# Transposing c2q alone: a change to the cross attention of a decoder layer on one core

## The chip, the core and the metric

The kernel runs on one core of a Trainium2 chip. The metric is device time in microseconds (us), the median of the runs made. A core has five engines with a queue each: TensorE (PE; its weight loads are listed apart as PEld), VectorE (DVE), ScalarE (ACT), GpSimd (POOL) and SyncE (SP), which here issues all DMAs. Each works through its instructions in the order in which they are written, and waits at semaphores.

## What is computed

A decoder layer in float32 over x (32 batches, 112 tokens, width 256) and a context (32 batches, 375 rows, width 256): self attention over channels, a cross attention, and a mixture of eight experts with a shared one. The change is in the cross attention, cut here to its core (c is the normalised state, q the context):

```python
cq = jnp.einsum('bcd,bqd,d->bcq', c, q, w_cq) + b_cq
s = (c @ w_c + b_c)[:, :, None] + (q @ w_q + b_q)[:, None, :] + cq
a = jax.nn.softmax(s, axis=2)
c2q_att = jnp.einsum('bcq,bqd->bcd', a, q)
b_att = jax.nn.softmax(jnp.max(s, axis=2), axis=1)
q2c_att = jnp.einsum('bc,bcd->bd', b_att, c)[:, None, :]
x = jnp.concatenate([c, c2q_att, c * c2q_att, c * q2c_att], axis=-1)
z = x @ W_l.T + b_l
```

## The kernel before

The kernel has two stages. The first runs both attentions in eight groups of four batches; a batch of a group is called a stream, j = 0 to 3. The first and the last group are written out, the six between are a loop, so they run the same instructions. The second stage runs the experts over blocks of 512 tokens; the change doesn't touch it.

Every float32 product is made of three in a faster type: each operand is split into a high part (a rounded copy, made by ScalarE) and a low part (the operand minus its high part, made by VectorE, for the context by GpSimd), and `mm3` (lines 74 to 78) takes low x high, high x low and high x high. So an operand passes through a bank of PSUM, ScalarE, VectorE and back to TensorE.

The order on each engine is written out by hand in that engine's `group`. At the end of a group this is done for each stream:

- `c2q_product` (L487, line numbers L76 to L78 in the trace, tiles ctx_hi, ctx_lo and op_hi, op_lo): the attention weights by the context, 9 products of 256 columns, into the stream's bank.
- L751 on ScalarE: c2q is scaled by the sum of exponentials and copied into `tmp`. L1126 on VectorE: c2q times c, into the other half of `tmp` (semaphore `x3_ok`, c_c2q_ready).
- `turn_x` (L499): four transposes of 128 columns each, of c2q and of c*c2q, into the stream's bank. L759 and L1138: high and low part of all four, 448 columns in one instruction each.
- `z_c2q` (L502): 12 products of 256 columns with two of the four blocks of W_l, added up in `z_bank`.

Between them stand other steps. `turn_h_pair` (L374) transposes the next group's normalised input hh, which VectorE makes in `normalise_h` (L921). The b_att chain goes over the four streams: m4, a transpose (L556), its maximum (L1121), the exponential (L754), `mrow` (L1133), a transpose back (L565), `b4` (L1142), and then eight small products (L571) that give q2c. ScalarE has `residual` (L602, four activations for the next group) between the last `a_high` (L679) and the first copy of c2q, and `context_hi` (L608, L609) of the next group's first stream after the second L759. GpSimd waits for the last x3_ok and then makes the low parts of that context (L822, L827). The last group has no next one: it has no `residual` and no `turn_h_pair`, but `moments3` (L147 to L156, the next stage's norm) on VectorE.

`c` transposed is kept in `ct`, as [128, stream, 2, 112], since z's first block needs it.

Of the kernel before, what the change touches and what calls it, by code (L numbers as in the profile page):

```python
# [26 lines left out]
ALU = mybir.AluOpType  # L27
# [23 lines left out]
def decoder_layer(nc, x, ctx, ctx_t, norm_w, norm_b, qkv_wt, qk_b, v_b, proj_wt, proj_b, w_cq, b_cq, w_c, b_c,  # L51
# [29 lines left out]
    with outer:  # L81
# [102 lines left out]
        with ExitStack() as c1:  # L184
# [94 lines left out]
            c2q_mm, c2q_ok, x3_ok = sem("c2q_product"), sem("c2q_copied"), sem("c_c2q_ready")  # L279
            t_x, x_hi_ok, x_lo_ok = sem("x23_transposed"), sem("x23_hi_ready"), sem("x23_lo_ready")  # L280
# [81 lines left out]
            def _(pe):  # L362
# [39 lines left out]
                def group(i, last_group):  # L402
# [93 lines left out]
                    def turn_x(j):  # L496
                        pe.wait_ge(x3_ok, ev[j])
                        for k in range(2 * KB):
                            last = pe.transpose(bank[j][:, k * L:(k + 1) * L], tmp[j][0:L, k * P:(k + 1) * P], ident[0:L, 0:L])  # L499
                        last.then_inc(t_x, 1)  # L500

                    def z_c2q(j):  # L502
                        pe.wait_ge(x_lo_ok, ev[j])
                        for k in range(2 * KB):
# [69 lines left out]
                    z_c2q(1)  # L574
# [3 lines left out]
                    z_c2q(2)  # L578
                    z_c2q(3)
                    if last_group:  # L580
# [13 lines left out]
            def _(act):  # L594
# [30 lines left out]
                def group(i, last):  # L625
# [50 lines left out]

                    def a_high(j):
# [70 lines left out]
                    for j in range(G):  # L748
                        act.wait_ge(c2q_mm, ev[j])
                        act.wait_ge(sinv2_ok, ev[j])  # L750
                        act.activation(tmp[j][0:L, 0:D], bank[j][0:L, 0:D], ACT.Copy, scale=sinv2[:, j:j + 1]).then_inc(c2q_ok, 1)  # L751
                        if j == 2:
                            act.wait_ge(mneg_ok, i + 1)
                            act.activation(mexp[:, :], m_bank[0:G, 0:L], ACT.Exp, bias=mneg[:, :], accum_out=msum[:, :]).then_inc(mexp_ok, 1)  # L754
                    if not last:
                        h_high_pair(i + 1, 0)
                    for j in range(G):
                        act.wait_ge(t_x, ev[j])
                        act.activation(op_hi[j][:, 0:2 * KB * L], bank[j][:, 0:2 * KB * L], ACT.Copy).then_inc(x_hi_ok, 1)  # L759
                        if j == 1 and not last:  # L760
                            context_hi(i + 1, 0)
                        if j == 1 and last:
                            act.wait_ge(shared_in, 48)
                            act.activation(shared_hi[:, 0:GU + D], shared_f[:, :], ACT.Copy).then_inc(shared_hi_ok, 1)
# [137 lines left out]
            def _(dve):  # L902
# [39 lines left out]
                def group(i, last):  # L942
# [33 lines left out]

                    def a_low(j):
# [146 lines left out]
                    for j in range(G):  # L1124
                        dve.wait_ge(c2q_ok, ev[j])
                        dve.tensor_tensor(tmp[j][0:L, D:2 * D], tmp[j][0:L, 0:D], c[:, j, :], ALU.mult).then_inc(x3_ok, 1)  # L1126
                        if j == 0 and last:
                            moments3(dve, 0)
                        if j == 2:
                            dve.wait_ge(mexp_ok, i + 1)  # L1130
                            dve.reciprocal(minv[:, :], msum[:, :]).then_inc(minv_ok, 1)
                            dve.wait_ge(minv_ok, i + 1)
                            dve.tensor_scalar(mrow[:, :], mexp[:, :], minv[:, 0:1], None, ALU.mult).then_inc(mrow_ok, 1)  # L1133
                    if not last:
                        h_low_pair(i + 1, 0)
                    for j in range(G):
# [471 lines left out]
```

## Time and profile before

| | us |
|---|---|
| median of 3 runs | 758.57 |
| lowest, highest | 756.07, 758.85 |
| the profiled execution, its time | 759.8 |
| its span, first to last instruction | 758.0 |
| TensorE busy in it | 699.2 |
| VectorE, ScalarE, GpSimd busy | 500.4, 408.3, 347.4 |

Busy times of different engines overlap. A product on TensorE is listed with its latency (0.28 us for 256 columns), but the next one starts 0.117 us later, so the distance of starts is its cost in the queue. An idle time stands in brackets with the instruction that ended it.

### The profile page before, as it was taken

The numbers are of one execution on the slowest core, as the hardware profiler recorded it, in microseconds if no ns is written. First come the engines' busy times: TensorE is split into PE (matmuls) and PEld (weight loads), VectorE is DVE, ScalarE is ACT, GpSimd is POOL, SyncE is SP. The second block draws the span as 40 slices with busy tenths as digits, with TensorE's granted clock in tenths as the row PEclk, the third lists the DMA queues.
The fourth block names the chain that finished last, engine by engine and source line by source line (L and its number), as shares of the span: only waits on it lengthen the run. The fifth ranks groups of instructions, "written<-read, shape, count | busy, mean of one in ns | idle before, by whom it ended". The sixth has DMA issues, their size and how long they took to land. (4 is left out here: it accounts for less than half of the span.)

```text
span 758.0 us, 13311 instructions
## 1 busy us (share of the span) xinstructions
PE 699.2 (92%) x4496; PEld 616.8 (81%) x4496; DVE 500.4 (66%) x1232; ACT 408.3 (54%) x923; POOL 347.4 (46%) x482
## 2 busy tenths in 40 slices
PE   3879999999999999999999865989999999999997
PEld 2768888988988898889888854878888888888886
DVE  5686685775875866758758654766576667666442
ACT  4855766776776768567767532524243333333321
POOL 2756846765657558557575311323222223232222
PEclk9989999999999999999999998999999999999999
DMA  7622322313213313223001057022221203121200
GB/s 215 180 87 69 117 69 66 108 38 98 88 48 88 98 47 99 65 70 117 24 22 37 18 148 266 1 112 83 112 84 58 108 31 138 55 112 57 112 29 29
DMA packets 50769, 64.47 MB, mean 85 GB/s; under 512 B 3801, under 2 KB 49417, under 8 KB 49841
## 3 DMA queue, kind: packets, MB, share of 16 engines
q1 hardware_dynamic: 50736, 64.06, 26.7%
q8 instruction: 18, 0.29, 0.2%
q14 instruction: 15, 0.11, 0.0%
HBM read 56.60 MB, written 7.45 MB: 85 GB/s over the span
## 5 line engine op out<-in xcount | busy, mean ns | idle before, releaser
L1440 POOL TENSOR_TENSOR sg<-sg,cw_wide 128x512 f32<-128x512 f32 x56 | 74.6, 1331 | 187.9 <-ACT sg L1397 177.7
L1401 ACT ACTIVATE a_hi<-af 128x512 fp32r<-128x512 f32 x63 | 39.8, 632 | 157.4 <-DVE af L1521 157.4
L76 PE MATMUL bank<-h_hi,w_lo 128*128 128x512 f32 x224 | 92.6, 413 | 6.9 <-DVE w_lo L1538 5.1
L77 PE MATMUL bank<-h_lo,w_hi 128*128 128x512 f32 x224 | 90.5, 404 | 0.0
L78 PE MATMUL bank<-h_hi,w_hi 128*128 128x512 f32 x224 | 89.6, 400 | 0.0
L822 POOL TENSOR_TENSOR ctxt_lo<-ctxtf,ctxt_hi 128x375 fp32r<-128x375 f32 x64 | 58.4, 933 | 64.3 <-ACT ctx_hi L609 56.2
L1521 DVE TENSOR_TENSOR af<-bank,sg 128x512 f32<-128x512 f32 x63 | 43.2, 686 | 65.0 <-POOL sg L1440 61.9
L1526 DVE TENSOR_TENSOR a_lo<-af,a_hi 128x512 fp32r<-128x512 f32 x63 | 47.2, 749 | 34.9 <-ACT a_hi L1401 34.9
L827 POOL TENSOR_TENSOR ctx_lo<-ctxf,ctx_hi 125x256 fp32r<-125x256 f32 x96 | 68.9, 746 | 0.0
L76 PE MATMUL bank<-w_hi,a_lo 128*128 128x256 f32 x224 | 63.3, 283 | 0.0
L77 PE MATMUL bank<-w_lo,a_hi 128*128 128x256 f32 x224 | 63.2, 282 | 0.0
L78 PE MATMUL bank<-w_hi,a_hi 128*128 128x256 f32 x224 | 63.2, 282 | 0.0
L76 PEld LDWEIGHTS bank<-h_hi,w_lo 128*128 128x128 f32 x224 | 43.4, 194 | 17.9 <-DVE w_lo L1538 5.5
L78 PEld LDWEIGHTS bank<-h_hi,w_hi 128*128 128x128 f32 x224 | 43.6, 195 | 10.2
L77 PEld LDWEIGHTS bank<-h_lo,w_hi 128*128 128x128 f32 x224 | 43.7, 195 | 7.8
L1003 DVE TENSOR_TENSOR op_lo<-bank,op_hi 112x512 fp32r<-112x512 f32 x32 | 22.1, 692 | 36.5 <-ACT op_hi L630 36.5
L1397 ACT ACTIVATE sg<-bank 128x512 f32<-128x512 f32 x63 | 37.1, 589 | 14.2 <-PE bank L78 13.9
L76 PEld LDWEIGHTS bank<-w_hi,a_lo 128*128 128x128 f32 x224 | 42.5, 190 | 2.5 <-DVE a_lo L1526 0.2
L77 PEld LDWEIGHTS bank<-w_lo,a_hi 128*128 128x128 f32 x224 | 42.6, 190 | 2.3
L78 PEld LDWEIGHTS bank<-w_hi,a_hi 128*128 128x128 f32 x224 | 42.6, 190 | 0.0
L76 PE MATMUL bank<-wp_hi,op_lo 128*128 128x256 f32 x128 | 38.5, 301 | 2.3 <-DVE wp_lo L1044 1.5
L76 PE MATMUL bank<-wl_hi,op_lo 128*112 128x256 f32 x128 | 37.8, 296 | 1.1 <-DVE op_lo L1138 1.1
(252 smaller groups left out, 2293.3 us busy)
## 6 DMA issues: line engine op xcount, KB each, us to landing
cw_wide<-cw_scratch SPq DMA_DIRECT2D x7, 2048.0 KB, 7.1
ctxtf<-in_ctx_t SPq DMA_DIRECT2D x32, 375.0 KB
ctxf<-in_ctx SPq DMA_DIRECT2D x32, 375.0 KB
xt<-in_x SPq DMA_DIRECT2D x8, 448.0 KB, 3.7
x_scratch<-x2b SPq DMA_DIRECT2D x8, 448.0 KB, 3.2
x2n<-x_scratch SPq DMA_DIRECT2D x7, 512.0 KB, 4.7
x2t<-x_scratch SPq DMA_DIRECT2D x7, 512.0 KB, 3.9
out_dram<-x2t SPq DMA_DIRECT2D x7, 512.0 KB, 2.9
```

The lines of the kernel that those rows point to most:

```text
L76: pe.matmul(dst, a_lo, b_hi, start=first, stop=False, **kw)
L77: pe.matmul(dst, a_hi, b_lo, start=False, stop=False, **kw)
L78: return pe.matmul(dst, a_hi, b_hi, start=False, stop=last, **kw)
L822: last_lo = pool.tensor_tensor(ctxt_lo[:, j, k, 0:S], ctxtf[:, j, k, :], f32(ctxt_hi[:, j, k, 0:S]), ALU.subtract)
L827: last_lo = pool.tensor_tensor(ctx_lo[:, j, b, :], ctxf[0:SB, j, b, :], f32(ctx_hi[:, j, b, :]), ALU.subtract)
L1003: dve.tensor_tensor(op_lo[j][0:L, :], bank[j][0:L, :], f32(op_hi[j][0:L, :]), ALU.subtract).then_inc(qk_lo_ok, 1)
L1397: act.activation(sg[b][:, :], g_bank[b][:, :], ACT.Silu).then_inc(sg_ok, 1)
L1401: act.activation(a_hi[n % (AHEAD + 1)][:, :], af[(p + n) % 2][:, :], ACT.Copy).then_inc(a_hi_ok, 1)
L1440: pool.tensor_tensor(sg[b][:, :], sg[b][:, :], cw_wide[p][:, ORDER[n], :], ALU.mult).then_inc(sgw_ok, 1)
L1521: dve.tensor_tensor(af[b][:, :], u_bank[b][:, :], sg[b][:, :], ALU.mult).then_inc(af_ok, 1)
L1526: dve.tensor_tensor(a_lo[b][:, :], af[(p + n) % 2][:, :], f32(a_hi[b][:, :]), ALU.subtract).then_inc(a_lo_ok, 1)
```

## The change

Only c2q is transposed (two transposes per stream). c*c2q is then made by VectorE from the transposed c2q in the bank and `ct`, straight in the transposed layout. Its high and low part are instructions of their own, from `tmp`, and `z_c2q` is divided into `z_c2q` and `z_x3` with six products each. GpSimd's wait for x3_ok stays as it was written. The order on TensorE, ScalarE and VectorE is written anew.

```diff
                     def turn_x(j):
-                        pe.wait_ge(x3_ok, ev[j])
-                        for k in range(2 * KB):
+                        pe.wait_ge(c2q_ok, ev[j])
+                        for k in range(KB):
                             last = pe.transpose(bank[j][:, k * L:(k + 1) * L], tmp[j][0:L, k * P:(k + 1) * P], ident[0:L, 0:L])
...
+                    def z_x3(j):
+                        pe.wait_ge(x3_lo_ok, ev[j])
+                        for k in range(KB, 2 * KB):
...
                     c2q_product(2)
+                    turn_x(0)
                     c2q_product(3)
+                    turn_x(1)
                     if not last_group:
                         turn_h_pair(i + 1, 0)
-                    turn_x(0)
-                    turn_x(1)
+                    z_c2q(0)
+                    turn_x(2)
                     pe.wait_ge(mrow_ok, i + 1)
-                    turn_x(2)
+                    turn_x(3)
                     pe.transpose(m_bank[0:L, P:P + G], mrow[:, :], ident[0:G, 0:G]).then_inc(t_b, 1)
-                    turn_x(3)
-                    z_c2q(0)
+                    z_c2q(1)
+                    z_x3(0)
                     pe.wait_ge(b4_ok, i + 1)
...
-                    z_c2q(1)
+                    z_c2q(2)
+                    z_x3(1)
                     if not last_group:
                         pe.wait_ge(h_lo_ok, G * (i + 1) + 2)
                         turn_h_pair(i + 1, 1)
-                    z_c2q(2)
                     z_c2q(3)
+                    z_x3(2)
+                    z_x3(3)
...
+                    def c2q_copy(j):
+                        act.wait_ge(c2q_mm, ev[j])
+                        act.wait_ge(sinv2_ok, ev[j])
+                        act.activation(tmp[j][0:L, 0:D], bank[j][0:L, 0:D], ACT.Copy, scale=sinv2[:, j:j + 1]).then_inc(c2q_ok, 1)
+
+                    def x_high(j):
+                        act.wait_ge(t_x, ev[j])
+                        act.activation(op_hi[j][:, 0:KB * L], bank[j][:, 0:KB * L], ACT.Copy).then_inc(x_hi_ok, 1)
+
+                    def x3_high(j):
+                        act.wait_ge(x3_ok, ev[j])
+                        act.activation(op_hi[j][:, KB * L:2 * KB * L], tmp[j][:, D:D + KB * L], ACT.Copy).then_inc(x3_hi_ok, 1)
...
+                    c2q_copy(0)
+                    c2q_copy(1)
+                    x_high(0)
+                    c2q_copy(2)
+                    act.wait_ge(mneg_ok, i + 1)
+                    act.activation(mexp[:, :], m_bank[0:G, 0:L], ACT.Exp, bias=mneg[:, :], accum_out=msum[:, :]).then_inc(mexp_ok, 1)
+                    x_high(1)
+                    c2q_copy(3)
                     if not last:
                         h_high_pair(i + 1, 0)
...
+                    x3_high(0)
+                    x_high(2)
+                    x3_high(1)
+                    x_high(3)
+                    if not last:
+                        context_hi(i + 1, 0)
...
+                    x3_high(2)
+                    x3_high(3)
...
+                    def x_low(j):
+                        dve.wait_ge(x_hi_ok, ev[j])
+                        dve.tensor_tensor(op_lo[j][:, 0:KB * L], bank[j][:, 0:KB * L], f32(op_hi[j][:, 0:KB * L]),
+                                          ALU.subtract).then_inc(x_lo_ok, 1)
+
+                    def x3_product(j):
+                        dve.wait_ge(x_hi_ok, ev[j])
+                        dve.tensor_tensor(tmp[j][:, D:D + KB * L].rearrange("p (k t) -> p k t", k=KB),
+                                          bank[j][:, 0:KB * L].rearrange("p (k t) -> p k t", k=KB), ct[:, j, :, :], ALU.mult).then_inc(x3_ok, 1)
+
+                    def x3_low(j):
+                        dve.wait_ge(x3_hi_ok, ev[j])
...
+                    x_low(0)
+                    x3_product(0)
+                    if last:
+                        moments3(dve, 0)
+                    dve.wait_ge(mexp_ok, i + 1)
+                    dve.reciprocal(minv[:, :], msum[:, :]).then_inc(minv_ok, 1)
+                    x_low(1)
+                    dve.wait_ge(minv_ok, i + 1)
+                    dve.tensor_scalar(mrow[:, :], mexp[:, :], minv[:, 0:1], None, ALU.mult).then_inc(mrow_ok, 1)
+                    x3_product(1)
                     if not last:
                         h_low_pair(i + 1, 0)
...
+                    x3_low(0)
+                    x_low(2)
+                    x3_product(2)
+                    dve.wait_ge(t_b, i + 1)
+                    dve.tensor_copy(b4[:, :], m_bank[0:L, P:P + G]).then_inc(b4_ok, 1)
+                    x3_low(1)
+                    x_low(3)
+                    x3_product(3)
+                    x3_low(2)
+                    x3_low(3)
```

In these pieces the name in brackets is the semaphore that the instruction waits for (a_transposed is `t_a`, c2q_copied `c2q_ok`, c_c2q_ready `x3_ok`, b_att_rows `mrow_ok`, x23_lo_ready `x_lo_ok` before and c2q_lo_ready the same after). TensorE in the loop's group before, from the last context product of stream 3 to the first weight product:

```order
L78 MATMUL bank3<-ctx_hi,op_hi3 112x256
L370 REGISTER_ALU
L374 MATMUL bank7<-ident,h3 128x112 [waits hh_ready]
L374 MATMUL bank7<-ident,h3 128x112 x3
L499 MATMUL bank0<-ident,tmp 128x112 [waits c_c2q_ready]
L499 MATMUL bank0<-ident,tmp 128x112 x3
L499 MATMUL bank1<-ident,tmp 128x112 [waits c_c2q_ready]
L499 MATMUL bank1<-ident,tmp 128x112 x3
L499 MATMUL bank2<-ident,tmp 128x112 [waits c_c2q_ready,b_att_rows]
```

TensorE there after the change, from the last context product of stream 2:

```order
L78 MATMUL bank2<-ctx_hi,op_hi2 112x256
L500 MATMUL bank0<-ident,tmp 128x112 [waits c2q_copied]
L500 MATMUL bank0<-ident,tmp 128x112
L76 MATMUL bank3<-ctx_hi,op_lo3 112x256 [waits a_lo_ready,context_lo_ready]
...
L78 MATMUL bank3<-ctx_hi,op_hi3 112x256
L500 MATMUL bank1<-ident,tmp 128x112 [waits c2q_copied]
L500 MATMUL bank1<-ident,tmp 128x112
L371 REGISTER_ALU
L375 MATMUL bank7<-ident,h3 128x112 [waits hh_ready]
L375 MATMUL bank7<-ident,h3 128x112 x3
L76 MATMUL bank4<-wl_hi,op_lo0 112x256 [waits c2q_lo_ready]
```

The first transposes of c2q stand ahead of the nine products of stream 3, and the first weight product ahead of the transposes of stream 2. ScalarE in the same group after the change:

```order
L704 ACTIVATE op_hi3<-bank3 125x336 [waits a_transposed]
...
L614 ACTIVATE x2n<-xt,ln1 112x256 [waits x1_ready]
L614 ACTIVATE x2n<-xt,ln1 112x256 x3
L692 ACTIVATE tmp<-bank0,sinv2 112x256 [waits sim_inv_sum,c2q_product]
L692 ACTIVATE tmp<-bank1,sinv2 112x256 [waits sim_inv_sum,c2q_product]
L696 ACTIVATE op_hi0<-bank0 128x224 [waits c2q_transposed]
L692 ACTIVATE tmp<-bank2,sinv2 112x256 [waits sim_inv_sum,c2q_product]
L778 ACTIVATE mexp,msum<-bank6,mneg 4x112 [waits m_max]
L696 ACTIVATE op_hi1<-bank1 128x224 [waits c2q_transposed]
L692 ACTIVATE tmp<-bank3,sinv2 112x256 [waits sim_inv_sum,c2q_product]
```

The four residual activations (L614, L602 before) stand ahead of the first copy of c2q as they did; the high parts now stand between the copies. VectorE there after the change:

```order
L950 TENSOR_SCALAR h3<-xt,mv1,ln1 112x256 x3
L1008 TENSOR_TENSOR op_lo0<-bank0,op_hi0 128x224 [waits c2q_hi_ready]
L1013 TENSOR_TENSOR tmp<-bank0,ct 128x224 [waits c2q_hi_ready]
L1173 RECIPROCAL minv<-msum 4x1 [waits m_exp]
L1008 TENSOR_TENSOR op_lo1<-bank1,op_hi1 128x224 [waits c2q_hi_ready]
L1176 TENSOR_SCALAR mrow<-mexp,minv 4x112 [waits m_inv_sum]
L1013 TENSOR_TENSOR tmp<-bank1,ct 128x224 [waits c2q_hi_ready]
```

Before, three products c*c2q stood between the normalised hh and minv, and all low parts behind mrow; now the low part of stream 1 stands ahead of mrow.

## Rows read from the trace of the kernel before

**Rows 1.** Windows: stretch, length, busy PE, PEld, DVE, ACT, POOL; clock; DMA.

```profile
115.44:166.99 51.55, 49.61 (x356) 44.99 (x354) 36.27 (x96) 35.97 (x91) 32.70 (x52) 1.00 0.26 78
218.54:270.08 51.54, 49.58 (x357) 44.99 (x354) 36.27 (x96) 35.96 (x91) 32.70 (x52) 1.00 0.27 77
```

**Rows 2.** Timeline, weight loads, a middle group: start, length, instruction, count, [idle before].

```profile
218.54 0.18 PEld L76 LDWEIGHTS bank<-ctx_hi,op_lo 125*112 125x112 f32 x1
...
219.85 0.17 PEld L76 LDWEIGHTS bank<-ctx_hi,op_lo 125*112 125x112 f32 x1 [0.21 <-issue]
...
221.15 0.39 PEld L374 LDWEIGHTS bank<-ident,h 112*128 112x128 f32 x4 [0.20 <-DVE h L921]
...
222.13 0.78 PEld L499 LDWEIGHTS bank<-ident,tmp 112*128 112x128 f32 x8 [0.59 <-DVE tmp L1126]
...
223.17 0.39 PEld L499 LDWEIGHTS bank<-ident,tmp 112*128 112x128 f32 x4 [0.26 <-DVE mrow L1133]
...
224.64 0.17 PEld L76 LDWEIGHTS bank<-wl_hi,op_lo 128*112 128x112 f32 x1 [0.40 <-DVE op_lo L1138]
...
226.03 1.87 PEld L571 LDWEIGHTS bank<-b,c 112*128 112x128 f32 x16
...
227.82 0.18 PEld L76 LDWEIGHTS bank<-wl_hi,op_lo 128*112 128x112 f32 x1
...
232.46 0.18 PEld L76 LDWEIGHTS bank<-wqkv_hi,h_lo 128*112 128x112 f32 x1
```

**Rows 3.** Timeline of the same stretch, ScalarE: residual and copies of c2q.

```profile
219.09 2.07 ACT L602 ACTIVATE x2n<-xt,ln 112x256 f32<-112x256 f32 x4
...
221.06 1.18 ACT L751 ACTIVATE tmp<-bank,sinv 112x256 f32<-112x256 f32 x3
```

**Rows 4.** Groups by form, 60 to 435: count | busy us, mean ns | idle.

```profile
L1138 DVE TENSOR_TENSOR op_lo<-bank,op_hi 128x448 fp32r<-128x448 f32 x32 | 19.0, 616 | 6.4 <-ACT op_hi L759 6.4
...
L751 ACT ACTIVATE tmp<-bank,sinv 112x256 f32<-112x256 f32 x32 | 13.1, 458 | 0.5 <-PE bank L78 0.5
...
L993 DVE TENSOR_TENSOR c_lo<-bank,c_hi 128x224 fp32r<-128x224 f32 x28 | 10.8, 386 | 7.0 <-ACT c_hi L662 7.0
...
L661 ACT ACTIVATE ct<-bank 128x224 f32<-128x224 f32 x28 | 9.9, 354 | 21.2 <-PE bank L458 21.2
```

**Rows 5.** Timeline of the middle group, VectorE: hh and mrow.

```profile
219.83 1.91 DVE L921 TENSOR_SCALAR h<-xt,mv,ln 112x256 f32<-112x256 f32 x4
...
222.85 0.27 DVE L1133 TENSOR_SCALAR mrow<-mexp,minv 4x112 f32<-4x112 f32 x1
```

**Rows 6.** Timeline of the middle group, GpSimd: context low parts of streams 0 and 1.

```profile
225.71 1.80 POOL L822 TENSOR_TENSOR ctxt_lo<-ctxtf,ctxt_hi 128x375 fp32r<-128x375 f32 x2 [4.77 <-ACT ctx_hi L609]
...
232.07 1.92 POOL L822 TENSOR_TENSOR ctxt_lo<-ctxtf,ctxt_hi 128x375 fp32r<-128x375 f32 x2 [2.48 <-ACT ctx_hi L609]
```

**Rows 7.** Timeline of the first group: copy of c2q and first transposes.

```profile
65.28 1.17 ACT L751 ACTIVATE tmp<-bank,sinv 112x256 f32<-112x256 f32 x3
...
66.66 1.95 PEld L499 LDWEIGHTS bank<-ident,tmp 112*128 112x128 f32 x12 [1.42 <-DVE tmp L1126]
```

**Rows 8.** Windows, columns as in rows 1: first, a middle and the last group.

```profile
64.00:67.00 3.00, 1.40 (x11) 0.97 (x11) 3.00 (x7) 3.00 (x9) 2.12 (x3) 0.99 0.05 18
67.00:70.00 3.00, 3.00 (x17) 2.70 (x16) 2.71 (x8) 2.80 (x6) 0.00 (x0) 0.50 0.52 153
...
221.00:224.00 3.00, 2.56 (x20) 1.84 (x19) 2.96 (x11) 3.00 (x10) 0.00 (x0) 1.00 0.28 60
...
427.00:430.00 3.00, 2.06 (x17) 1.64 (x16) 2.93 (x14) 1.59 (x6) 1.06 (x2) 1.00 0.00 0
```

**Rows 9.** Timeline of the last group: norm statistics and transposes.

```profile
426.92 1.39 DVE L152 BATCH_NORM_STATS2 st<-x2n 128x6 f32<-128x256 f32 x4
...
429.15 0.39 PEld L499 LDWEIGHTS bank<-ident,tmp 112*128 112x128 f32 x4 [1.05 <-DVE tmp L1126]
...
430.53 0.60 PE L499 MATMUL bank<-ident,tmp 112*128 112x112 f32 x4
```

More of the change, by code:

```diff
@@ L278, in decoder_layer @@
             t_a, a_hi_ok, a_lo_ok = sem("a_transposed"), sem("a_hi_ready"), sem("a_lo_ready")
[L279 to L280 removed]
+            c2q_mm, c2q_ok = sem("c2q_product"), sem("c2q_copied")
+            t_x, x_hi_ok, x_lo_ok = sem("c2q_transposed"), sem("c2q_hi_ready"), sem("c2q_lo_ready")
+            x3_ok, x3_hi_ok, x3_lo_ok = sem("c_c2q_ready"), sem("c_c2q_hi_ready"), sem("c_c2q_lo_ready")
             t_m, mneg_ok, mexp_ok, minv_ok, mrow_ok = sem("m_transposed"), sem("m_max"), sem("m_exp"), sem("m_inv_sum"), sem("b_att_rows")
@@ L503, in z_c2q @@
                         pe.wait_ge(x_lo_ok, ev[j])
-                        for k in range(2 * KB):
+                        for k in range(KB):
+                            t = slice(k * L, (k + 1) * L)
+                            mm3(pe, z_of(j), op_hi[j][:, t], op_lo[j][:, t], wl_hi[:, KB + k, :], wl_lo[:, KB + k, :], False, False,
+                                skip_group_check=True)
+                    def z_x3(j):
+                        pe.wait_ge(x3_lo_ok, ev[j])
+                        for k in range(KB, 2 * KB):
                             t = slice(k * L, (k + 1) * L)
@@ L747, in group @@
                         residual(i + 1)
[L748 to L754, printed above, removed]
+                    c2q_copy(0)
[6 more added lines that the diff above has]
+                    c2q_copy(3)
                     if not last:
                         h_high_pair(i + 1, 0)
[L757 to L764, printed above, removed]
+                    x3_high(0)
[4 more added lines that the diff above has]
+                        context_hi(i + 1, 0)
+                    else:
+                        act.wait_ge(shared_in, 48)
+                        act.activation(shared_hi[:, 0:GU + D], shared_f[:, :], ACT.Copy).then_inc(shared_hi_ok, 1)
+                    x3_high(2)
+                    x3_high(3)
                     if last:
@@ L1123, in group @@
                         normalise_h(i + 1)
[L1124 to L1133, printed above, removed]
+                    x_low(0)
[8 more added lines that the diff above has]
+                    x3_product(1)
                     if not last:
                         h_low_pair(i + 1, 0)
-                    for j in range(G):
-                        dve.wait_ge(x_hi_ok, ev[j])
-                        dve.tensor_tensor(op_lo[j][:, 0:2 * KB * L], bank[j][:, 0:2 * KB * L], f32(op_hi[j][:, 0:2 * KB * L]),
-                                          ALU.subtract).then_inc(x_lo_ok, 1)
-                        if j == 0:
-                            dve.wait_ge(t_b, i + 1)
-                            dve.tensor_copy(b4[:, :], m_bank[0:L, P:P + G]).then_inc(b4_ok, 1)
+                    x3_low(0)
[8 more added lines that the diff above has]
+                    x3_low(3)
                     dve.wait_ge(q2c_mm, i + 1)
```

2 lines of the change are left out of this document (added).

## The prediction

> **What bounds the kernel now.** I read the page's busy times first (TensorE leads them by far), then the table of windows over whole groups, then the timeline of one middle group. The groups of the first stage repeat with a period of 51.55 us, 49.6 of them with TensorE busy, ScalarE and VectorE near 36 [rows 1]. So a saving counts only if it lands in TensorE's queue, and a wait on TensorE costs its full length. The change lies between the third context product and the next group's first product, 218.54 to 232.46 in the group shown [rows 2]. The brackets of the weight-load rows there are the moments when the queue stood: 0.21 (a_low of the fourth stream), 0.20 (hh), 0.59 (the c*c2q product of VectorE), 0.26 (mrow) and 0.40 (the first low part), 1.66 in all. From 226.03 on nothing stands: the 0.117 us from one 256-column product to the next ((226.03 - 224.64)/12) is kept up to 232.46. The six groups between the first and the last are alike (the window rows differ by a few hundredths).
>
> **What is removed.** Each stream needs two transposes instead of four, 8 fewer per group. Eight loads of them took 0.78 us in the queue [rows 2], so 0.78 us per group goes from TensorE, with nothing beside it. The 48 weight products, the 18 context products and the small b_att products stay.
>
> **What is moved, and the new wait.** turn_x(0) now stands ahead of the fourth context product, and it waits for the first c2q copy of ScalarE. ScalarE has the four residual activations in front of that copy: they run from 219.09, and the copy starts at 221.06 and takes 0.46, that is until 221.52 [rows 3, 4]. A release reaches TensorE after 0.05 (mrow: 222.85 + 0.27 = 223.12, load at 223.17) [rows 2, 5]. The third context product is issued by 218.54 + 9 x 0.117 = 219.59. So TensorE stands from 219.59 to 221.57: **1.98 us of new wait, with 9 products (1.05 us) queued behind it** that before ran in just this stretch. This is what the change pays.
>
> Then, in TensorE's order: transposes of stream 0 to 221.77, fourth context product to 222.82, transposes of stream 1 to 223.02, the pair of h (hh is ready at 219.83 + 1.91 = 221.74 [rows 5]) to 223.43, first half of z for stream 0 (6 products, 0.70) to 224.13. Its low part is ready long before: transposes done 221.98, high copy to 222.4, low part to 222.8 (0.35 and 0.39, the nearest rows of 128x224 [rows 4]). Transposes of stream 2 to 224.33. For stream 3 mrow is needed: transposes of stream 1 end near 223.3 (four take 0.60 from first to last, and a pair 0.2 less [rows 9]), high copy to 223.67, low part to 224.10, and mrow, queued 0.3 behind its start, 224.0 + 0.27, released at 224.33. So the old wait of 0.26 is just gone. Stream 3 and b_att to 224.67, first half of stream 1 to 225.37. The second half of stream 0 needs VectorE's queue: x3 product 1 from 224.2, h_low_pair to 225.1, x3_low(0) 225.07 to 225.46, released 225.51: a wait of 0.14. Then 226.21; b4 is copied by 226.14, so the b_att products start on time and take 1.79 (226.03 to 227.82 [rows 2]), to 228.00; five half products (3.51) and the second pair of h (0.41) end at 231.92. Before it was 232.46. That is 0.54 us less; the small gaps around the b_att transpose that I passed over (about 0.1) leave **0.45 us per middle group**. By sums: 0.78 removed, waits 2.12 where there were 1.66, and 0.1 of small gaps.
>
> **The cover of the extra instructions.** ScalarE gets 8 high copies of 224 columns for 4 of 448, VectorE 8 low parts and 4 products for 4 and 4. On VectorE 448 columns took 616 ns and 224 took 386 [rows 4]: the halves are 0.16 dearer per stream by duration. What hides them is TensorE's saturated stretch from 226 on. It doesn't hide the part before b4, where five VectorE instructions in a row lead to x3_low(0); if each starts 0.1 later than I have it, the group loses 0.5 and the gain is gone. Both ends for this term: no wait at all (gain 0.6) and 0.5 later (gain -0.05); I take the value that the start-to-start spacing gives, since four 256-column instructions on VectorE took 1.91 us together [rows 5] and not four times their duration. The Trainium skill ("VectorE: DVE Perf Modes", section on the TRN2 errata) speaks against this change: each VectorE or ScalarE instruction pays a fixed latency, and small tiles pay it each time, so one should cut tiles large. The durations here agree; by the rule taken in full, without overlap between neighbours, five instructions would come 0.08 later each and the middle group would gain 0.05 instead of 0.45.
>
> Context work: ScalarE's context_hi(0) moves behind x_high(3), to about 225.3, and GpSimd waits for it and for the last x3 product: it starts its four microseconds near 227 instead of 225.71. It ends near 231.1, and its next piece waits for ScalarE until 232.07 anyway [rows 6]. SP's load of that stream's context is issued 1.3 us later, with most of a group in hand. Nothing is added on SP.
>
> **First group.** The copy starts at 65.28 there, so TensorE would stand from 62.9 to 65.8, 2.9 us; before it stood in pieces, the longest 1.42, and the clock then fell [rows 7, 8]. The same walk from 65.78 ends at 76.15 at full clock, 77.7 with one stretch at half clock; before 77.95. I take +0.3, ends -0.8 (a fall at the worst place) and 1.8 (none).
>
> **Last group.** No residuals: the copy is ready as the third context product ends, so no new wait. But moments3 (1.39 for the statistics, about half a us for the rest) now stands ahead of mrow for stream 1 on VectorE, mrow comes at 430.30, and TensorE stands 1.6 us before turn_x(3), where it stood 1.05 for the x3 product [rows 9]. The z products end 1.0 earlier; the last product with q2c waits for GpSimd's low part, and 0.6 is left (ends 0.2 and 1.0).
>
> **Sum.** Six middle groups x 0.45 = 2.7, first 0.3, last 0.6: 3.6 us. The profiled execution has a span of 758.0 and a time of 759.8, and would come to 756.2; the median of the three runs is 758.57, 1.2 below it, and I set the sum against that: **755.0 us**. A measurement of this kernel can tell about 0.5%, 3.8 us, from no change; my forecast lies just inside.
>
> **Rival 1, the clock (slower).** After the pause before the first group's transposes the granted clock stood at 0.50 from 67 to 70 [rows 8]: 1.2 instead of 2.4 GHz. Before it TensorE had stood 1.42 at a stretch [rows 7] and was busy for 1.40 of 3 us, with a few transposes [rows 8]. The last group's 1.05 brought no fall, nor do the short waits of the middle group [rows 8, 9]. My new wait of 1.98 in each of six groups is longer than both. Against a fall: products run right up to it and 1.05 us of products follow close behind, where in the first group only transposes stood on both sides of the pause; but in the 3 us from 219.6 TensorE would be busy for 1.0 to 1.3, no more than there, so it is a near thing. Price: 3 us at half clock do 1.5 us of work less, of which little is cover here. One fall in every middle group is 6 x 1.5 = 9 against a gain of 3.6: 764.0, slower. In half of them: 759.5. It decides from the third fall on; from the fifth it is slower than 0.5%. The Trainium skill ("TensorE: Matmul & The Clock Gate", the table "Why this matters for your kernels") asks that idle gaps between bursts be avoided for this reason; no row of the middle groups shows it yet.
>
> **Rival 2, VectorE's queue is the bound.** The low parts, mrow and b4 come 0.5 late in each group, as above: the middle groups' 2.7 is gone, 757.7. For it: VectorE is busy for 2.96 of 3 us from 221 to 224 already [rows 8]. Against it: the spacing just told.
>
> **Rival 3, the waits fit better.** If the fourth context product and the transposes absorb what follows (no wait for x3_low, none of the small gaps, and the first group keeps its clock), middle groups gain 0.7 and the whole comes to 4.2 + 1.8 + 1.0 = 7.0: 751.6. What it can't do is run without the 1.98, since ScalarE's order fixes that.
>
> **How the numbers follow.** Forecast 0.50; rival 1 in some groups 0.19, in all 0.06; rival 2 0.12; rival 3 0.13. Forecast range 753 to 757.5. For 8 in 10 I go from 751.2 to 760.0, which leaves out all-group falls and a third of rival 3. Faster by over 0.5% (below 754.8): 0.13 and a little over half of the forecast's 0.50, 0.40. Slower by over 0.5%: all groups' falls and a few of the some, 0.10. Within: 0.50.
>
> **What would show it.** Middle groups of 51.1 us instead of 51.55; a wait of about 2.0 us ahead of the first c2q transposes in each of six, released by the c2q copy; no wait for mrow; one under 0.3 for the low part of c*c2q; clock 1.00 in all middle groups. A clock below 1.00 there is rival 1; waits of 0.4 and more for x3_low or b4 are rival 2. I am wrong at the root if ScalarE's copy comes before its residuals, or if the wait is not 2 us.

## The result: 753.67 us, 4.95 us less

The median of 20 runs of the changed kernel is 753.67 us (750.0 to 757.1), against 758.62 us (755.9 to 761.75) of 20 runs of the kernel before on the same chips. The ratio is 0.993, with a 95% interval from 0.9913 to 0.9948: faster by 0.65%. The profiled execution has a span of 752.1 us, where it was 758.0.

The busy line of the page after (line 1 under its first heading) reads:

```profile
PE 688.1 (91%) x4432; PEld 611.3 (81%) x4432; DVE 513.3 (68%) x1264; ACT 413.2 (55%) x955; POOL 349.4 (46%) x482
```

TensorE still leads by far. The window over a whole middle group, from b_att transpose to b_att transpose, with the columns of [rows 1]:

```profile
217.71:268.75 51.04, 48.01 (x349) 44.20 (x347) 37.97 (x100) 36.63 (x95) 33.07 (x52) 1.00 0.26 78
```

Where [rows 1] had 51.55, a middle group now takes 51.03 to 51.04. TensorE's busy time fell by 1.6 and the period by 0.5; busy time counts each product with its latency, so it overstates what left the queue (eight transposes cost 0.75 there, as an experiment below shows). VectorE and ScalarE are busier by 1.7 and 0.7, which costs nothing here. The clock is 1.00. The timeline of weight loads in a middle group shows the waiting (columns as in [rows 2], and the same moment of the group: its b_att transpose is at 217.71, in [rows 2] at 218.54):

```profile
220.74 0.20 PEld L500 LDWEIGHTS bank<-ident,tmp 112*128 112x128 f32 x2 [1.93 <-ACT tmp L692]
...
225.39 1.87 PEld L581 LDWEIGHTS bank<-b,c 112*128 112x128 f32 x16
...
231.11 0.18 PEld L76 LDWEIGHTS bank<-wqkv_hi,h_lo 128*112 128x112 f32 x1
```

The five brackets of [rows 2], 1.66 in all, have become a single one of 1.93 ahead of the first transposes, released by ScalarE's copy of c2q. From the b_att transpose to the next group's first product it is 13.40 us, where it was 13.92 [rows 2]: 0.52 per group. ScalarE's rows say why the copy is where it is:

```profile
218.26 2.07 ACT L614 ACTIVATE x2n<-xt,ln 112x256 f32<-112x256 f32 x4
220.23 0.82 ACT L692 ACTIVATE tmp<-bank,sinv 112x256 f32<-112x256 f32 x2
```

As in [rows 3], the four residuals stand in front of it. Three places make up 3.84 of the 4.95 us. The first group gave 0.35 (16.00 to 15.65 from its b_att transpose to the next group's first product), six middle groups 6 x 0.52 = 3.12, the last one 0.37 (16.81 to 16.44 to its logits). About 1.1 us of the medians' difference lies outside of these stretches; it is taken up below.

### The profile page after: what moved, and what is told of

Its sections match the earlier page's. It is cut to its first block and busy times, and to the rows that moved or that the text cites. A ratio compares the mean times of both kernels' runs of the same rounds, so it can differ in the third digit from the quotient of the medians.

```text
span 752.1 us, 13247 instructions
## 1 busy us (share of the span) xinstructions
PE 688.1 (91%) x4432; PEld 611.3 (81%) x4432; DVE 513.3 (68%) x1264; ACT 413.2 (55%) x955; POOL 349.4 (46%) x482
## 5 line engine op out<-in xcount | busy, mean ns | idle before, releaser
L851 POOL TENSOR_TENSOR ctxt_lo<-ctxtf,ctxt_hi 128x375 fp32r<-128x375 f32 x64 | 59.5, 951 | 64.1 <-DVE tmp L1013 37.5
```

The costliest lines, as they stand in the source:

```text
L851: last_lo = pool.tensor_tensor(ctxt_lo[:, j, k, 0:S], ctxtf[:, j, k, :], f32(ctxt_hi[:, j, k, 0:S]), ALU.subtract)
```

## Experiments

Two readings of the result stood at the start. **The layout reading**: the layout alone is worth much more than 0.52 per group, and most of it is paid back at one wait, 1.93 us behind the residuals. **The order reading**: the layout is worth its 0.78 of transposes and little else, and what counts is the order of the queues, by which the kernel before could gain as much. A third question was how near the new wait is to a fall of the clock.

**Moving the residuals.** ScalarE's four residual activations go behind the last high copy of the group:

```diff
                     a_high(3)
-                    if not last:
-                        residual(i + 1)
                     c2q_copy(0)
 ...
                     x3_high(3)
+                    if not last:
+                        residual(i + 1)
```

> The changed kernel with ScalarE's four residual activations moved from before the first copy of c2q to behind the last x3_high; same work. Theory (the change's price is the 1.9 us that TensorE stands for that copy in each middle group, because of the residuals): the wait goes, TensorE then waits about 0.7 us for hh of VectorE instead, middle groups fall from 51.03 to about 49.7 us, and with 1.5 to 2 us more from the first group the median falls by about 10 to 744. Rival (the wait only takes up slack that VectorE's queue of low parts would leave anyway): mrow or x3_low is late by nearly as much, groups stay within 0.2 of 51.03, median 752 to 754.

Measured: 742.41 us (5 runs; ratio 0.979, 0.9772 to 0.9807; this ratio and those that follow are to runs of the kernel before, made beside). The group's window, what is left of waiting on TensorE in it (timeline of weight loads), and the residuals, now in ScalarE's free time (timeline of ScalarE):

```profile
210.84:260.60 49.76, 48.10 (x348) 44.27 (x346) 37.52 (x100) 36.75 (x95) 33.08 (x52) 1.00 0.27 80
```

```profile
214.43 0.17 PEld L76 LDWEIGHTS bank<-wl_hi,op_lo 128*112 128x112 f32 x1 [0.55 <-DVE op_lo L1008]
```

```profile
218.39 2.07 ACT L614 ACTIVATE x2n<-xt,ln 112x256 f32<-112x256 f32 x4
221.20 0.55 ACT L634 ACTIVATE h_hi<-bank 128x448 fp32r<-128x448 f32 x1 [0.74 <-PE bank L375]
```

The wait of 1.93 is gone, and 0.55 has come in its place: the first low part (L1008) stands behind the four hh instructions on VectorE. The group takes 49.77, 1.26 less than in the changed kernel. The residuals cost nothing where they now are: ScalarE waits for TensorE for 0.74 right behind them. Of the 11.3 us that the medians differ, the six groups give 7.6. In the profiled runs another 2.5 come from the first group, which has no stretch at half clock here, and 1.9 from ahead of it, where this run has one such stretch and the changed kernel two.

**The same move without the change.** In the kernel before, the residuals go behind its last high copy of the transposed operands:

```diff
                     a_high(3)
-                    if not last:
-                        residual(i + 1)
                     for j in range(G):
                         act.wait_ge(c2q_mm, ev[j])
 ...
                         if j == 1 and not last:
                             context_hi(i + 1, 0)
+                    if not last:
+                        residual(i + 1)
```

> The kernel before with the residual activations moved behind the last high part of x. Theory: before the change the first transposes of c2q waited for VectorE (hh, then c*c2q), not for ScalarE's copy, so it gains nothing that counts: 0 to 0.1 us per group, median 758 to 758.6. Rival (the residuals bound the kernel before as well, and the move is worth the same in both): 1 us or more per group, median under 752.

Measured: 759.06 us (12 runs, ratio 1.0003, 0.9986 to 1.002), groups of 51.51 (window below, columns as in [rows 1]), with the waits of [rows 2] as before (0.23 for hh, 0.59, 0.26, 0.33).

```profile
218.69:270.22 51.53, 49.60 (x356) 44.98 (x354) 36.26 (x96) 36.46 (x91) 32.80 (x52) 1.00 0.25 77
```

So ScalarE's order was no limit in the kernel before. It became one by the change, which moved the reader of the copy forward and left the residuals ahead of the copy.

**Only the place of turn_x(0).** The fourth context product goes back ahead of the first transposes, so that its nine products run in the stretch that the wait leaves empty:

```diff
                     c2q_product(2)
-                    turn_x(0)
                     c2q_product(3)
+                    turn_x(0)
                     turn_x(1)
```

> The changed kernel with the transposes of stream 0 put back behind the fourth context product on TensorE; same work. Theory: 9 products (1.05 us) run inside the wait, the wait shrinks to about 0.7, but mrow and the low part of stream 0 are then waited for (0.3 and 0.2), so 0.35 us per middle group comes back, 51.03 to 50.7, median near 751. Rival (TensorE's place of the transposes doesn't matter, the end is set by ScalarE and VectorE behind the copy): no change, 753.7. A third outcome, over 0.9 us per group, would say that the walk's waits for VectorE are wrong.

Measured: 752.73 us (6 runs, ratio 0.9916, 0.9897 to 0.9935), groups of 50.66. Its window and the waits in its queue:

```profile
216.51:267.17 50.66, 48.78 (x348) 44.27 (x346) 37.98 (x100) 36.48 (x95) 33.08 (x52) 1.00 0.26 79
```

```profile
217.82 0.17 PEld L76 LDWEIGHTS bank<-ctx_hi,op_lo 125*112 125x112 f32 x1 [0.21 <-issue]
...
219.53 0.20 PEld L500 LDWEIGHTS bank<-ident,tmp 112*128 112x128 f32 x2 [0.61 <-ACT tmp L692]
219.89 0.20 PEld L500 LDWEIGHTS bank<-ident,tmp 112*128 112x128 f32 x2 [0.16 <-ACT tmp L692]
...
220.82 0.17 PEld L76 LDWEIGHTS bank<-wl_hi,op_lo 128*112 128x112 f32 x1 [0.34 <-DVE op_lo L1008]
```

The wait shrinks from 1.93 to 0.61, but only 0.37 of the 1.32 reaches the period. The transposes of stream 1 now come right behind those of stream 0 and wait 0.16 for their own copy, the first low part is late by 0.34, and a_low of the fourth stream by 0.21, as before the change. The six groups give 2.2 us together and the medians differ by 0.9: in the last group TensorE waits 0.89 and 1.64, where the changed kernel waits 1.47. A wait that is taken away on a full queue uncovers the next one.

**Transposes put back, unused.** Each pair of transposes runs twice, on the same source into the banks' other halves; nothing else changes, and the second results aren't read:

```diff
-                        for k in range(KB):
-                            last = pe.transpose(bank[j][:, k * L:(k + 1) * L], tmp[j][0:L, k * P:(k + 1) * P], ident[0:L, 0:L])
+                        for k in range(2 * KB):
+                            last = pe.transpose(bank[j][:, k * L:(k + 1) * L], tmp[j][0:L, (k % KB) * P:(k % KB + 1) * P], ident[0:L, 0:L])
```

> The changed kernel with each pair of c2q transposes issued twice (four per stream, as many as before the change; the second pair's result isn't used). Theory: the transposes are on the path for their full 0.1 us each, so 0.78 us per group comes back and a little for the later release of the high part: middle groups 51.8 to 52.0, median 760. Rival (they were hidden in waits): under 0.3 us per group, 754 to 756.

Measured: 760.85 us (12 runs, ratio 1.0029, 1.001 to 1.0047), groups of 51.78:

```profile
220.15:271.94 51.79, 48.77 (x356) 44.97 (x354) 37.82 (x100) 36.74 (x95) 33.03 (x52) 1.00 0.25 77
```

Eight transposes cost 0.75 per group on the path, where the prediction had 0.78. With them the changed order is slower than the kernel before. The order and the halves alone, as the change has them, lose 0.23 per group.

**How near the clock is.** Behind the residuals, ScalarE makes one copy more (or three) of a bank that is ready, into a part of tmp that nothing reads, so that the wait ahead of turn_x(0) is longer and nothing else is added to TensorE:

```diff
                     if not last:
                         residual(i + 1)
+                        act.wait_ge(c2q_mm, ev[1])
+                        act.wait_ge(sinv2_ok, ev[0])
+                        for n in range(1):
+                            act.activation(tmp[n][0:L, D:2 * D], bank[0][0:L, 0:D], ACT.Copy, scale=sinv2[:, 0:1])
                     c2q_copy(0)
```

> The changed kernel with one more ScalarE copy of 256 columns (into a part of tmp that is not in use) ahead of the first copy of c2q in all groups but the last: TensorE stands 0.36 us longer there, 2.3 instead of 1.93. If the clock is far from falling: every middle group 51.03 + 0.36 = 51.4, clock 1.00 in all, median +2.5, 756.2. If the changed kernel stands at the edge of a fall (rival 1 of the prediction, near): some of the six middle groups show a stretch at 0.50 and are 1 us or more longer than the others, median 758 or more.

> The same with three more copies: TensorE stands 1.08 us longer, 3.0. Far from a fall: middle groups 52.1, clock 1.00, median +7.6, 761.3. At the edge or beyond: more middle groups with a stretch at 0.50 than with one copy, each 1 to 1.7 us longer, median 764 to 769.

Measured: 757.85 us (10 runs, ratio 0.9983, 0.9967 to 0.9999) with one copy, where the wait is 2.29; 764.36 us (4 runs, ratio 1.0083, 1.0058 to 1.0107) with three, where it is 3.01. The window rows of three middle groups with one copy (the one between the first two rows took 52.83, at 0.97 too):

```profile
112.13:164.98 52.85, 49.46 (x349) 45.55 (x346) 37.79 (x100) 37.19 (x96) 32.98 (x52) 0.97 0.25 76
...
217.81:269.18 51.37, 47.98 (x349) 44.20 (x346) 37.88 (x100) 36.95 (x96) 33.00 (x52) 1.00 0.25 78
269.18:322.05 52.87, 49.48 (x349) 45.56 (x347) 37.82 (x100) 37.16 (x96) 32.98 (x52) 0.97 0.25 75
```

Four of the six middle groups fell. A fallen group has a mean clock of 0.97 and is 1.48 longer than the one that did not fall (52.85 against 51.37). In the timeline, the wait itself is 2.29 in the fallen group (first two rows) and in the other (last two); the same transposes behind it take 0.78 in the one and 0.45 in the other:

```profile
115.52 0.20 PEld L500 LDWEIGHTS bank<-ident,tmp 112*128 112x128 f32 x2 [2.29 <-ACT tmp L692]
...
118.90 0.78 PEld L500 LDWEIGHTS bank<-ident,tmp 112*128 112x128 f32 x4
...
221.20 0.20 PEld L500 LDWEIGHTS bank<-ident,tmp 112*128 112x128 f32 x2 [2.29 <-ACT tmp L692]
...
223.70 0.45 PEld L500 LDWEIGHTS bank<-ident,tmp 112*128 112x128 f32 x4
```

The window right behind that wait shows TensorE busy for all of it at the lower level (0.50, that is 1.2 GHz):

```profile
117.00:120.00 3.00, 3.00 (x18) 2.72 (x15) 1.97 (x7) 1.85 (x6) 0.00 (x0) 0.50 0.44 141
```

With three copies every second group fell:

```profile
114.49:168.13 53.64, 49.54 (x349) 45.74 (x347) 37.85 (x100) 37.95 (x98) 33.07 (x52) 0.97 0.25 75
168.13:220.21 52.08, 47.97 (x348) 44.17 (x346) 37.94 (x100) 37.71 (x98) 33.05 (x52) 1.00 0.25 77
```

So a wait of 1.93 brought no fall in 12 middle groups of two profiles, one of 2.29 brought four in six, and one of 3.01 three in six. In the middle groups the changed kernel stands 0.36 us of ScalarE's time away from rival 1. The clock did not fall more often behind the longer wait, against what was expected of three copies. In the first group it is even the other way round: it fell behind a wait of 2.69 and of 2.70 in the two profiles of the changed kernel, and not behind 2.74 with one copy or 3.45 with three. A first group that keeps its clock is worth about 1.5 us, which fits a median just below the 758 that was expected with falls. So the length of the wait alone doesn't decide; what else does (where in time the wait begins, for one) no run here settles.

**The changed kernel once more.** It was run once more beside the two above, to compare places rather than times:

> The changed kernel once more, unchanged, for one profile: where two executions of the same instructions differ. If the 2 us by which the second stage was shorter in the first profile of it (329.7 from the last group's b_att transpose to the end, 332.7 before) belong to the change, it is 329 to 330 again; if they come from where the granted clock falls in the second stage, it lies anywhere from 329 to 333, and the first stage repeats within 0.1 us per group.

Measured: 753.98 us in one run, middle groups of 50.96 to 51.00 and half-clock stretches at the same places of the program as in the first profile. The periods repeat to 0.1%.

**Splitting hh.** After the residuals were moved, the wait left over was 0.55, for a low part behind four hh instructions. Here VectorE does the hh of streams 0 and 1 at the old place, those of streams 2 and 3 behind x3_low(1), and the statistics of the last group behind its last low part, on top of the moved residuals (normalise_h takes the half as a second argument, and waits at the first half only):

```diff
-                        normalise_h(i + 1)
+                        normalise_h(i + 1, 0)
                     x_low(0)
                     x3_product(0)
-                    if last:
-                        moments3(dve, 0)
 ...
                     x3_low(1)
+                    if not last:
+                        normalise_h(i + 1, 1)
                     x_low(3)
                     x3_product(3)
                     x3_low(2)
                     x3_low(3)
+                    if last:
+                        moments3(dve, 0)
```

> The version with the residual activations late, with two more moves on VectorE: the second half of normalise_h (streams 2 and 3, needed only for the second pair of transposes) goes behind x3_low(1), and in the last group moments3 goes behind the last x3_low. Theory: what TensorE waits for in resid_late is the low part of stream 0, 0.55 us behind normalise_h, and in the last group 1.47 us for mrow behind moments3; the first wait goes in six groups (49.76 to about 49.3), 0.5 to 1 us more in the first, up to 1 us in the last, median 738 to 739. Rival (GpSimd's context work, released by the last x3 product, or h_low_pair becomes late in its place): groups stay at 49.7 or more, median 742.

Measured: 742.23 us (6 runs, ratio 0.9766, 0.9741 to 0.979). The middle groups take 49.17 and have no wait over 0.2 in this stretch. But the time is that of the moved residuals. The profiled run reaches its first b_att transpose 2.2 later than theirs, with two stretches at half clock ahead of it for one, and the last group gives back 2.9 (weight loads):

```profile
411.57 0.20 PEld L500 LDWEIGHTS bank<-ident,tmp 112*128 112x128 f32 x2 [0.36 <-DVE mrow L1175]
...
421.67 0.86 PEld L131 LDWEIGHTS bank<-ident,h 128*128 128x128 f32 x8 [2.83 <-DVE h L164]
```

The statistics behind the last low part make the third norm late, and TensorE stands 2.83 us at the entry to the next stage. From the last b_att transpose to the end of the program it takes 333.05, against 329.72 in the changed kernel. The statistics cost 1.47 ahead of mrow and 2.83 at the end; so they went between, behind x3_low(1):

```diff
                     x3_low(1)
                     if not last:
                         normalise_h(i + 1, 1)
+                    else:
+                        moments3(dve, 0)
 ...
                     x3_low(3)
-                    if last:
-                        moments3(dve, 0)
```

> split_hh with moments3 of the last group moved up again, behind x3_low(1) instead of behind the last x3_low. Theory: in split_hh the middle groups came to 49.15 us, but moments3 was so late that the next stage's transposes waited 2.8 us for it; here that wait goes, and the stretch from the last group's b_att transpose to the end shrinks from 333 to 329 to 330; median 738 to 739.5. Rival (the last group's loss is elsewhere, and only moved): 741 or more.

Measured: 738.83 us (5 runs, ratio 0.9739, 0.9725 to 0.9753). This is the fastest version here, with 329.44 from the last b_att transpose to the end, 19.8 us under the kernel before and 14.8 under the changed one. Its middle group, and the two waits left in its last one:

```profile
209.99:259.12 49.13, 47.81 (x348) 44.20 (x346) 37.98 (x100) 36.77 (x95) 33.21 (x52) 1.00 0.26 81
```

```profile
411.02 0.20 PEld L500 LDWEIGHTS bank<-ident,tmp 112*128 112x128 f32 x2 [0.35 <-DVE mrow L1175]
...
420.31 0.17 PEld L76 LDWEIGHTS bank<-wl_hi,cw_lo 128*112 128x112 f32 x1 [1.08 <-POOL cw_lo L865]
```

**The same order on the old layout.** To tell the two readings apart, the kernel before got both moves as well: residuals late, and hh in two halves, the second behind the copy of b4.

```diff
                     a_high(3)
-                    if not last:
-                        residual(i + 1)
 ...
-                        normalise_h(i + 1)
+                        normalise_h(i + 1, 0)
 ...
                             dve.tensor_copy(b4[:, :], m_bank[0:L, P:P + G]).then_inc(b4_ok, 1)
+                            if not last:
+                                normalise_h(i + 1, 1)
```

> The kernel before (four transposes per stream, c*c2q made ahead of them) with the two moves that paid in the changed one: residual activations late, second half of normalise_h behind b4. It tells what the new layout is worth once the queues are in order. Theory: VectorE's hh and c*c2q still stand ahead of the transposes and the high and low parts of 448 columns behind them, so TensorE still waits 0.8 us or so for the first low part; middle groups 50.6 to 50.8 against 49.15, median near 751. Rival (the layout is worth only its 0.78 us of transposes): middle groups 49.9 to 50.0, median near 745.

Measured: 753.93 us (6 runs, ratio 0.9938, 0.9921 to 0.9955), groups of 50.82, just over the upper end that was expected. Window and waits:

```profile
216.08:266.89 50.81, 49.34 (x356) 44.94 (x354) 36.23 (x96) 36.32 (x91) 32.70 (x52) 1.00 0.26 79
```

```profile
217.39 0.17 PEld L76 LDWEIGHTS bank<-ctx_hi,op_lo 125*112 125x112 f32 x1 [0.21 <-issue]
...
218.69 0.39 PEld L374 LDWEIGHTS bank<-ident,h 112*128 112x128 f32 x4 [0.21 <-DVE h L922]
...
220.07 0.39 PEld L499 LDWEIGHTS bank<-ident,tmp 112*128 112x128 f32 x4 [0.22 <-DVE mrow L1134]
...
221.47 0.17 PEld L76 LDWEIGHTS bank<-wl_hi,op_lo 128*112 128x112 f32 x1 [0.33 <-DVE op_lo L1139]
```

The order alone brings the old layout 0.73 per group, as much in the whole as the change did. With the same two moves the new layout takes 49.17. So under this order the layout is worth 50.82 - 49.17 = 1.65 per group, where its eight transposes cost 0.75. That the rest comes from halves that let TensorE start on a stream earlier is argued, not shown by a run of its own.

How much a better order would still find in the old layout was not tried. The four waits left in it are 0.97 together; without any of them it would take 49.85, still 0.68 above 49.17. The layout reading holds for the orders tried. Of the order reading this much is true: what the change got as it stands, 51.03, the order alone gets too.

## Why the prediction was right, and where it was off

**The new wait** was predicted at 1.98 us, from the residuals' place, and measured at 1.93; the first transposes start 3.03 behind the b_att transpose, which is 221.57 - 218.54, the predicted one. That the residuals are its cause is shown by the run that moves them.

**The walk through a middle group** held almost step by step. Taking 0.83 off its times (217.71 against 218.54), it puts the b_att products at 225.38 and they are at 225.39; the next group at 231.09 and it is at 231.11; mrow ready at 223.44. VectorE's rows:

```profile
223.16 0.26 DVE L1176 TENSOR_SCALAR mrow<-mexp,minv 4x112 f32<-4x112 f32 x1
...
224.26 0.38 DVE L1018 TENSOR_TENSOR op_lo<-tmp,op_hi 128x224 fp32r<-128x224 f32 x1
...
225.16 0.15 DVE L1184 COPY b<-bank 112x4 f32<-112x4 f32 x1
```

mrow is ready at 223.42, x3_low(0) starts at 224.26 where the walk had 224.24, and b4 ends at 225.31 where it had 225.31. The predicted wait of 0.14 for x3_low(0) came to only 0.04; the rest had already passed ahead of the transpose of mrow. The deduction of about 0.1 for small gaps, taken from the walk's 0.54, was the mis-sized term: the group gained 0.52, against 0.45. The prediction's check "by sums" doesn't bear out its 0.45: 0.78 less the added waits (2.12 - 1.66) is 0.32, and 0.42 with the gaps. With the measured waits it is 0.78 - (1.93 + 0.04 - 1.66) = 0.47. The wait for mrow is gone, as said.

**The cover of the extra instructions** held. The value taken, spacing and not duration, is the one that the rows confirm: from the start of x3_low(0) to that of b4, three instructions of 0.38 took 0.90, or 0.30 each. So rival 2 didn't come. The Trainium skill's rule ("VectorE: DVE Perf Modes", section on the TRN2 errata), read without overlap of neighbours, would by the prediction's estimate have left 0.05 per group. The measured 0.52 is against that reading.

**GpSimd's context work** was forecast "near 227", that is 226.2 here, and started at 226.37; its next piece still waits for ScalarE, as in [rows 6], for 0.87:

```profile
226.37 1.94 POOL L851 TENSOR_TENSOR ctxt_lo<-ctxtf,ctxt_hi 128x375 fp32r<-128x375 f32 x2 [6.25 <-DVE tmp L1013]
```

What the prediction did not see is what this work does to VectorE beside it (last section). It cost nothing: TensorE shows no wait for the two slow low parts.

**First group**: +0.3 predicted, 0.35 measured, with one stretch at half clock as in the middle case of its bounds (wait 2.69 for the copy; the windows stand against [rows 8]):

```profile
66.15 0.20 PEld L500 LDWEIGHTS bank<-ident,tmp 112*128 112x128 f32 x2 [2.69 <-ACT tmp L692]
```

```profile
64.00:67.00 3.00, 0.84 (x7) 0.85 (x8) 2.63 (x5) 2.86 (x8) 2.47 (x4) 1.00 0.12 41
67.00:70.00 3.00, 3.00 (x20) 3.00 (x19) 2.20 (x7) 2.18 (x7) 0.00 (x0) 0.59 0.55 146
```

**Last group**: 0.6 predicted, 0.37 measured. The mechanism was right: the statistics stand ahead of mrow and TensorE waits for it, 1.47 where 1.6 was said.

```profile
424.94 1.39 DVE L152 BATCH_NORM_STATS2 st<-x2n 128x6 f32<-128x256 f32 x4
...
427.06 0.26 DVE L1176 TENSOR_SCALAR mrow<-mexp,minv 4x112 f32<-4x112 f32 x1
```

```profile
427.37 0.20 PEld L500 LDWEIGHTS bank<-ident,tmp 112*128 112x128 f32 x2 [1.47 <-DVE mrow L1176]
...
435.93 0.17 PEld L76 LDWEIGHTS bank<-wl_hi,cw_lo 128*112 128x112 f32 x1 [0.43 <-POOL cw_lo L865]
```

The mis-sized term is how much earlier the z products end: 0.82 (12.05 from the b_att transpose to the last one ahead of q2c's, where it was 12.87), and the step had 1.0. Of that, 0.48 is given back at the wait for GpSimd's low part, 0.43 in the row above, where the step had 0.4.

**Rival 1** did not come: clock 1.00 in all middle groups. "A near thing" was a fair weight: 0.36 us more of ScalarE's work made it come in four of six, at the price of about 1.5 each that was put on it. But only two executions were seen by group.

The Trainium skill ("TensorE: Matmul & The Clock Gate", the table "Why this matters for your kernels") asks that long idle gaps between bursts be avoided; the prediction left the word "long" out. The runs with the longer waits agree with the advice, in four and in three of six groups; the middle groups of the changed kernel, with their 1.93, don't show it.

**The sum** was 3.6 for the three kinds of group and came to 3.84. The forecast put the change just inside the half per cent that a measurement can tell from none; the measured 753.67 is just outside of that, and within the forecast's own range of 753 to 757.5. The 1.3 us between them has two parts: 0.24 from the groups, and the 1.1 that no step of the prediction had.

**What stays open** is this 1.1. In the second stage, whose instructions the change doesn't touch, the profiled pair differs by 2.6 us in favour of the changed kernel, which reached its first b_att transpose 0.5 later. Part of the 2.6 goes with a stretch at a lowered clock that the kernel before has near 498 and the changed one, whose second stage begins 3.3 earlier, doesn't have: the lead in the same instructions grows there from 4.3 to 5.9 and is back at 5.0 by 515. A window of before, then the one of after that is 3 us earlier (columns as in [rows 1]):

```profile
498.00:501.00 3.00, 3.00 (x11) 2.44 (x10) 2.30 (x3) 0.80 (x2) 0.74 (x1) 0.60 0.40 93
```

```profile
495.00:498.00 3.00, 3.00 (x21) 2.69 (x20) 1.57 (x3) 1.12 (x2) 0.89 (x1) 1.00 0.75 257
```

The stretch is there in the kernel before with its residuals moved, in the one with turn_x(0) behind, and with one copy more. It is missing in both profiles of the changed kernel, with the residuals moved, with the extra transposes (which is slower than before) and in the old layout with the new order. So it follows neither the time nor the layout, and one profile each is too few to call it the change's. Earlier in that stage it is the changed kernel whose clock is lower (0.76 on average from 439 to 475, against 0.86 from 442 to 478), and it gains there all the same. So the clock alone doesn't account for the 2.6, and where the second stage's falls come from stays open.

The 20 runs of the changed kernel say how much of this is chance: nine took 750.0 to 752.1 at a mean clock of 0.986 to 0.989, eleven 753.6 to 757.1 at 0.979 to 0.984. The median lies at the lower edge of the eleven, and both profiles (753.99 and 753.98, at 0.981) are among them. Where in the program the quicker nine kept their clock, no profile shows.

## What to carry to other kernels

When an operation is moved forward on the bound engine, follow its operand to the engine that makes it and look at what stands ahead of it in that queue: here four activations that nobody was waiting for turned a gain of 1.78 us per group (51.55 to 49.77) into 0.52. A change of layout and the order of the queues around it are one change: the order alone gave 0.73, the layout as placed 0.52, and both together 2.38 per group. Then go around once more, since each wait taken away uncovers the next (1.93, then 0.55, then none), and see to the last pass of the loop separately.

## What the runs showed of the hardware

**Low parts ran nearly three times slower beside GpSimd.** The subtraction L1018 has both operands in SBUF; it is 128x224. In the middle groups, L1018 of streams 2 and 3 took 1.17 and 1.04 us while GpSimd's L851 ran (1.06 and 1.05 in the first group). The 18 others of the run, without that work beside them, took 0.37 to 0.39. The rows of the changed kernel, first the operation by line (ns: min/median/max), then the timeline:

```profile
L1018 DVE TENSOR_TENSOR op_lo<-tmp,op_hi x32: 370/383/1168, 70.0 to 429.9; 128x224 fp32r<-128x224 f32 x32
```

```profile
226.43 2.13 DVE L1018 TENSOR_TENSOR op_lo<-tmp,op_hi 128x224 fp32r<-128x224 f32 x2 [0.22 <-ACT op_hi L700]
```

Low parts with one operand in a PSUM bank kept their time. In the kernel before, L1138 (128x448) ran beside the same work of GpSimd [rows 6] in 14 of its 32 instructions, at 0.61 to 0.63, where the others took 0.60 to 0.62:

```profile
226.09 1.16 DVE L1138 TENSOR_TENSOR op_lo<-bank,op_hi 128x448 fp32r<-128x448 f32 x2 [0.90 <-ACT op_hi L759]
```

In the changed kernel h_lo (L968, a bank too) took 0.62 beside it and without it; L1008 and L1013 never ran beside it. In the fastest version, one low part per group from SBUF ran beside GpSimd and took 0.95. Whoever puts these on the path should count on 1.1, not 0.38.

**The clock fell at waits that differ little.** The level fell to 1.2 GHz in four of six groups behind a wait of 2.29 and in none of twelve behind 1.93, each time for about 1.5 us of lost work. It did not fall more often behind 3.01 (three of six), and in the first group it fell behind 2.69 and not behind 3.45.
